# One VectorE instruction instead of two for the rests of a half of turned probabilities, and another layout of their buffer

## The chip, the cores and the metric

One core of a Trainium2 chip runs the whole program. The metric is the time of one execution on the device in microseconds. Five engines work side by side and meet through semaphores only: TensorE (PE in the rows; PEld is its weight load), VectorE (DVE), ScalarE (ACT), GpSimd (POOL), and SyncE (SP), which issues transfers.

## What is computed

A layer over 4 sequences of 2048 tokens with 256 features: "talking heads" attention with 16 heads of 16 features, whose logits and probabilities are each mixed over the heads, then a layer norm, a soft mixture of experts and a second layer norm. The attention is where the time goes:

```python
logits = jnp.einsum('bhid,bhjd->bhij', q, k) * SCALE
logits = jnp.einsum('bhij,gh->bgij', logits, Wpre)
attn = jax.nn.softmax(logits, axis=-1)
attn = jnp.einsum('bhij,gh->bgij', attn, Wpost)
out = jnp.einsum('bhij,bhjd->bhid', attn, v)
```

## The kernel before

**Tiles and slots.** A tile is 8 queries by 16 heads, which are the 128 partitions, against all 2048 keys. A sequence has 16 passes (`it`) of 16 tiles (`t`), so there are 4 × 16 × 16 = 1024 tiles. Every engine runs the same loop over slots, one slot per tile, and each works through its own list in the order in which the code is written; only semaphores tie them. In slot T the scores and the softmax of tile T are made, and the probabilities of tile T-2 are turned.

**A slot on each engine.** A slot has two halves, A (`hf` 0, the first 1024 keys) and B (`hf` 1).

- TensorE: `scores(T, 0)` (24 matmuls into `psS`), `turn(T-2, 0)` (48 small matmuls into `psP`), `scores(T, 1)`, `turn(T-2, 1)`. A turn multiplies the probabilities with the mixed post weights, so that keys become partitions. It fills both banks of `psP`: bank `ih` 0 takes the first four of the tile's eight queries, bank 1 the last four. There is one `psP`, so the next turn must wait until both banks are read (`s_ml`).
- ScalarE: for half A `mixed_high` of bank 0 and of bank 1 (line 694: `psP` rounded to float16, into the buffer `PT`, which is the tensor `big` in the rows), then `exps(T, 0)` (line 675) and `highs(T, 0)` (line 704); for half B the same with `exps(T, 1)`, `factor` (line 685) and `highs(T, 1)`.
- VectorE: `half_max(T, 0)` (line 867, 1024 scores), `recip` (898), `mixed_low` of bank 0 and of bank 1 for half A (line 878: what the rounding to float16 left over, `psP` minus the high part), `low(T-1, 1)` (line 906, 512 wide), `half_max(T, 1)`, `mixed_low` twice for half B, `low(T, 0)` (line 906, 1024 wide). `exps` waits for `half_max` (`s_nb`).
- GpSimd: mixed queries, softmax weights and a part of `low`.

Each `mixed_low(c)` waits for `mixed_high(c)` of its own bank (`s_mh`). So in a half four instructions read `psP`: ScalarE bank 0, ScalarE bank 1, VectorE bank 0, VectorE bank 1, and VectorE can be at bank 0 while ScalarE is at bank 1.

**Slots with more in them.** After 8 tiles `PT` is full, and TensorE multiplies it with the values (`output`, line 1282, 256 matmuls in four pieces) in the slots `t % 8 == 2`, the first piece already within the scores of half A. VectorE copies the result out (`out_copy`, line 889) in the slots `t % 8 == 3`. The row work (projection `y`, layer norm, routing) of earlier passes is put into slots by two tables:

```python
FIRST = dict(bias=1, y=4, residual=10, root1=(11, 4))
LATER = dict(norm=2, root2=(3, 4), turn_u=5, logits=6, keep=10, weigh=10, combine=10, turn_c=11)
```

Seven of the 16 slots of a pass (0, 7, 8, 12, 13, 14 and 15) hold none of this on TensorE or VectorE. They are called plain below.

## Time and profile before

| | |
|---|---|
| median of 3 runs | 8362.6 us (8351.86 to 8367.09) |
| profiled execution | 8358.64 us, its span 8356.8 us |
| TensorE busy | 7996.8 us, 96% of the span |
| VectorE busy | 7605.1 us, 91% |
| ScalarE busy | 6848.0 us, 82% |
| GpSimd busy | 6046.9 us, 72% |
| instructions of line 878 (VectorE) | 4096, mean 679 ns |

Busy shares tell which engines are near their limit on average; they don't tell which wait ends last in a given slot. Timelines list the start and the length of each instruction; two neighbours on one engine overlap in the records by their tails, so the pace of an engine is read from start to start. "x2" marks two merged instructions, whose length is that from the first's start to the second's end.

### The profile page before, as it was taken

What the parts mean: (1) busy time and instruction counts of PE and PEld (TensorE: products, weight loads), DVE (VectorE), ACT (ScalarE), POOL (GpSimd) and SP (SyncE); (2) the same over time, 40 slices, a digit from 0 to 9 for tenths busy, and PEclk for the clock granted to TensorE, in tenths of its full rate; (3) what the DMA queues carried; (4) which work ended last, traced back from release to release, by engine and by line L of the source; (5) the groups of instructions that cost most, each with busy time, mean ns of one, the idle gap of its engine ahead of it and who ended that gap; (6) DMA issues with size and microseconds to landing.
All of it is one profiled execution on the core that took longest, in us unless ns stands there. A gap on an engine that the chain in (4) does not pass through costs nothing.

```text
span 8356.8 us, 449859 instructions
## 1 busy us (share of the span) xinstructions
PE 7996.8 (96%) x182764; PEld 4649.9 (56%) x182764; DVE 7605.1 (91%) x13390; ACT 6848.0 (82%) x11648; POOL 6046.9 (72%) x12006
## 2 busy tenths in 40 slices
PE   7999999998899999999889999999979999999997
PEld 4555555555555555555545555555554555555554
DVE  7999999997899999999789999999978999999996
ACT  5888888886688888888568888888857888888884
POOL 6777777774677777777477777777737777777773
PEclk9999999998999999999899999999989999999998
DMA  1011111112101111111211111111121011011112
GB/s 53 23 28 27 26 26 27 26 27 91 34 24 27 27 26 26 27 28 26 89 35 25 26 27 26 27 26 27 26 88 36 25 26 28 25 27 26 27 26 93
DMA packets 265756, 284.04 MB, mean 34 GB/s; under 512 B 41089, under 2 KB 252673, under 8 KB 261377
## 3 DMA queue, kind: packets, MB, share of 16 engines
q1 hardware_dynamic: 263680, 255.07, 11.3%
q8 instruction: 1462, 23.95, 1.2%
q14 instruction: 614, 5.02, 0.2%
HBM read 78.75 MB, written 39.85 MB: 14 GB/s over the span
## 4 chain that ended last, share of the span: by engine, by line
PE 73%; DVE 12%; issue 10%; POOL 1%; ACT 1%; DVEq 1%; DMA 0%; SPq 0%; POOLq 0%; ACTq 0%
PE psS L1248 47%; PE psP L1267 15%; PE psO L1282 6%; DVE big L878 5%; DVE pl L906 2%; DVE spare L867 2%; PE psM L1293 1%; ACT big L694 1%; DVE ot L889 1%; PE psS L1378 1%; PE psM L1308 1%; PE psS L1407 1%; PE psS L1209 0%; DVE nb L867 0%; PE psS L1196 0%
## 5 line engine op out<-in xcount | busy, mean ns | idle before, releaser
L1248 PE MATMUL psS<-KH,AX 64*128 64x512 f16 x32768 | 3928.4, 377 | 52.0 <-DMA AX<-AX 50.1
L694 ACT ACTIVATE big<-psP 128x512 f16<-128x512 f32 x4096 | 2222.4, 595 | 826.2 <-PE psP L1267 822.9
L878 DVE SCALAR_TENSOR_TENSOR big<-psP,big 128x512 f16<-128x512 f32 x4096 | 2613.9, 679 | 175.5 <-ACT big L694 174.0
L675 ACT ACTIVATE pr<-psS,nb 128x1024 f32<-128x1024 f32 x2048 | 2289.7, 1118 | 192.9 <-DVE nb L867 190.1
L1248 PEld LDWEIGHTS psS<-KH,AX 64*128 64x128 f16 x32768 | 1451.5, 95 | 1513.5 <-DMA AX<-AX 51.7
L704 ACT ACTIVATE ph<-pr 128x1024 f16<-128x1024 f32 x2048 | 2166.8, 1058 | 32.3
L1248 PE MATMUL psS<-KL,AX 64*128 64x512 f16 x16384 | 2106.3, 377 | 0.0
L906 DVE TENSOR_TENSOR pl<-pr,ph 128x1024 f16<-128x1024 f32 (+1 forms) x2048 | 2078.3, 1015 | 0.0
L1267 PE MATMUL psP<-rh,ph 64*128 64x64 f16 x32768 | 1671.7, 191 | 131.4 <-DVE big L878 112.0
L1267 PEld LDWEIGHTS psP<-rh,ph 64*128 64x128 f16 x32768 | 1468.7, 95 | 557.9 <-DVE big L878 395.9
L1267 PE MATMUL psP<-rl,ph 64*128 64x64 f16 x32768 | 1667.0, 191 | 4.7 <-issue 4.3
L1267 PE MATMUL psP<-rh,pl 64*128 64x64 f16 x32768 | 1667.4, 191 | 4.0 <-issue 3.7
L567 POOL TENSOR_SCALAR tot<-sums,ff 128x1 f32<-128x1 f32 x1024 | 758.6, 741 | 1109.1 <-ACT ff L685 1104.9
L1267 PEld LDWEIGHTS psP<-rl,ph 64*128 64x128 f16 x32768 | 1463.1, 95 | 108.7 <-issue 6.1
L1267 PEld LDWEIGHTS psP<-rh,pl 64*128 64x128 f16 x32768 | 1463.6, 95 | 8.0 <-issue 7.4
L867 DVE CUSTOM_DVE_ANT_0 spare<-psS,lift 128x1024 f16<-128x1024 f32 x1024 | 1247.0, 1218 | 208.2 <-PE psS L1248 208.0
L867 DVE CUSTOM_DVE_ANT_0 spare<-psS,lift,nb 128x1024 f16<-128x1024 f32 x1024 | 1310.7, 1280 | 102.5 <-PE psS L1248 95.1
L1248 PEld LDWEIGHTS psS<-KL,AX 64*128 64x128 f16 x16384 | 806.8, 94 | 963.4 <-issue 3.4
L558 POOL TENSOR_TENSOR pl<-pr,ph 128x512 f16<-128x512 f32 x1024 | 1217.9, 1189 | 0.0
L486 POOL TENSOR_TENSOR at<-Q,wpre_q 128x128 f32<-128x128 f32 x2048 | 784.0, 402 | 6.9 <-POOL AX L499 5.0
L499 POOL TENSOR_TENSOR AX<-at,AX 128x256 f16<-128x256 f32 x1024 | 687.0, 671 | 2.6
L591 POOL CAST rh<-rp 128x128 f16<-128x128 f32 x1024 | 653.9, 639 | 7.6 <-POOL rp L582 6.5
(137 smaller groups left out, 6286.4 us busy)
## 6 DMA issues: line engine op xcount, KB each, us to landing
AX<-AX SPq DMA_DIRECT2D x2048, 64.0 KB, 2.0
ph<-in_xT SPq DMA_DIRECT2D x16, 512.0 KB, 8.7
xr<-in_x SPq DMA_DIRECT2D x64, 128.0 KB, 2.3
Q<-in_w SPq DMA_DIRECT2D x8, 1024.0 KB, 7.2
out<-V SPq DMA_DIRECT2D x16, 512.0 KB, 3.7
d_x<-x SPq DMA_DIRECT2D x60, 128.0 KB, 2.0
d_xn<-xn SPq DMA_DIRECT2D x60, 128.0 KB, 2.0
d_lg<-lg SPq DMA_DIRECT2D x60, 128.0 KB, 2.0
```

Of the source, the lines that this page charges most:

```text
L486: g.tensor_tensor(v, Q[:, :, bass.ds(i0, HQ)].unsqueeze(2).broadcast_to([P, KT, H, HQ]), wpre_q[:, :].unsqueeze(1).unsqueeze(3).broadcast_ ...
L499: g.tensor_tensor(AX[:, t % TG, 0:KT, 1, :], at[:, :, :], AX[:, t % TG, 0:KT, 0, :], ALU.subtract).then_inc(s_A, 1)
L558: g.tensor_tensor(pl[:, t % 2, NL:N], pr[:, t % 2, NL:N], ph[:, t % 2, NL:N], ALU.subtract).then_inc(s_plg, 1)
L567: g.tensor_scalar(tot[:, p:p + 1], sums[:, p, 0:1], ff[:, p, 0:1], sums[:, p, 1:2], ALU.mult, ALU.add).then_inc(s_tot, 1)
L675: a.activation(pr[:, p, h * N2:(h + 1) * N2], psS[:, 2 * h:2 * h + 2, :].rearrange("p c n -> p (c n)"), ACT.Exp, bias=nb[:, p, h:h + 1], s ...
L694: a.activation(PT[:, hf * JH:(hf + 1) * JH, :, 0, i0:i0 + HQ], psP[:, ih, :].rearrange("p (j g i) -> p j g i", j=JH, g=H), ACT.Copy, scale ...
L704: a.activation(ph[:, t % 2, cs], pr[:, t % 2, cs], ACT.Copy).then_inc(s_ph, 1)
L867: v.tensor_tensor_reduce(out=spare[:, :], in0=psS[:, 2 * h:2 * h + 2, :].rearrange("p c n -> p (c n)"), in1=lift[:, 0:1].broadcast_to([P, ...
L878: v.scalar_tensor_tensor(out=PT[:, js, :, 1, i0:i0 + HQ], in0=psP[:, ih, :].rearrange("p (j g i) -> p j g i", j=JH, g=H), scalar=MDROP, in ...
L906: v.tensor_tensor(pl[:, t % 2, cs], pr[:, t % 2, cs], ph[:, t % 2, cs], ALU.subtract)\
L1248: mm = pe.matmul(psS[:, 2 * hp + half, :], AX[rows, k8, kq, s_, :], K_[rows, kq, hp, :], start=n == 0, stop=n == len(steps) - 1, tile_posi ...
L1267: mm = pe.matmul(psP[:, ih, j * HP:(j + 1) * HP], p_[rows, t % 2, cs], r_[rows, t % 4, hf, :], start=n == 0, stop=n == 2, tile_position=(i ...
```

## The change

`mixed_low` is called once per half instead of twice. It waits until ScalarE has done both banks, and makes the rests of both banks in one instruction of 1024 elements per partition. For its output to be one regular pattern over both banks, the buffer `PT` is laid out anew: key half `f` and query half `h` come first, then key tile, head, high/rest, query. The other edits follow from that: the order of the queries inside a group of 64 changes (GpSimd reads `Q` at another offset), the output matmuls read their 128 columns as two runs of 64, `out_copy` writes its result back in two runs, and `s_ml` counts two per tile.

```diff
@@ -106,7 +106,7 @@
 
         big = sb("big", [P, JT * H * GI])
 
-        PT = big[:, :].bitcast(F16).rearrange("p (j g s i) -> p j g s i", j=JT, g=H, s=2)
+        PT = big[:, :].bitcast(F16).rearrange("p (f h j g s i) -> p f h j g s i", f=2, h=2, j=JH, g=H, s=2)
         KH = sb("KH", [P, KQ, NP, CW], F16)
         KL = sb("KL", [P, KQ, NP, CW], F16)
         V = sb("V", [P, JT, H, 2, HD], F16)
@@ -480,7 +480,7 @@
                         g.wait_ge(s_S, T * 2 - (TG - 1) * 2)
                     g.wait_ge(s_A, T * 4 + 1)
                     for h in range(2):
-                        i0 = it * (TI * QI) + (t * QI + h * HQ)
+                        i0 = it * (TI * QI) + t // TG * GI + h * (GI // 2) + t % TG * HQ
                         v = at[:, :, h * HP:(h + 1) * HP].rearrange("p k (g i) -> p k g i", g=H)
                         apart(g)
                         g.tensor_tensor(v, Q[:, :, bass.ds(i0, HQ)].unsqueeze(2).broadcast_to([P, KT, H, HQ]),
@@ -690,8 +690,8 @@
                     a.wait_ge(s_D, T * 2 + hf + 1 + 1)
                     if t % TG == 0:
                         a.wait_ge(s_F, Gd * NC + 2 * hf + 2)
-                    i0 = (t % TG) * QI + ih * HQ
-                    a.activation(PT[:, hf * JH:(hf + 1) * JH, :, 0, i0:i0 + HQ],
+                    i0 = (t % TG) * HQ
+                    a.activation(PT[:, hf, ih, :, :, 0, i0:i0 + HQ],
                                  psP[:, ih, :].rearrange("p (j g i) -> p j g i", j=JH, g=H),
                                  ACT.Copy, scale=MDROP).then_inc(s_mh, 1)
 
@@ -869,16 +869,13 @@
                                            op0=ALU.add, op1=ALU.min,
                                            accum_out=nb[:, t % 2, h:h + 1]).then_inc(s_nb, 1)
 
-                def mixed_low(T, t, c):
-
-                    v.wait_ge(s_mh, T * NC + c + 1 + 1)
-                    hf, ih = c // 2, c % 2
-                    i0 = (t % TG) * QI + ih * HQ
-                    js = slice(hf * JH, (hf + 1) * JH)
-                    v.scalar_tensor_tensor(out=PT[:, js, :, 1, i0:i0 + HQ],
-                                           in0=psP[:, ih, :].rearrange("p (j g i) -> p j g i", j=JH, g=H),
-                                           scalar=MDROP, in1=PT[:, js, :, 0, i0:i0 + HQ],
-                                           op0=ALU.mult, op1=ALU.subtract).then_inc(s_ml, 1)
+                def mixed_low(T, t, hf):
+
+                    v.wait_ge(s_mh, T * NC + 2 * hf + 2 + 1)
+                    i0 = (t % TG) * HQ
+                    high, rest = (PT[:, hf, :, :, :, k, i0:i0 + HQ].rearrange("p h j g i -> p (h j g) i") for k in range(2))
+                    v.scalar_tensor_tensor(out=rest, in0=psP[:, :, :].rearrange("p h (a i) -> p (h a) i", i=HQ),
+                                           scalar=MDROP, in1=high, op0=ALU.mult, op1=ALU.subtract).then_inc(s_ml, 1)
 
                 def out_copy(Gd, half, R, part):
 
@@ -886,8 +883,8 @@
                         v.wait_ge(s_F, (Gd + 1) * NC + NC)
                         v.wait_ge(s_y, R + 1)
                     qs = slice(part * GQ // 2, (part + 1) * GQ // 2)
-                    ins = v.tensor_reduce(ot[:, qs, half * GI:(half + 1) * GI],
-                                          psO[:, qs.start * P:qs.stop * P].rearrange("p (q s i) -> p q i s", s=2, i=GI),
+                    ins = v.tensor_reduce(ot[:, qs, half * GI:(half + 1) * GI].rearrange("p q (h i) -> p q h i", h=2),
+                                          psO[:, qs.start * P:qs.stop * P].rearrange("p (q h s i) -> p q h i s", h=2, s=2, i=GI // 2),
                                           X, ALU.add)
                     ins.then_inc(s_oc, 1)
 
@@ -1078,7 +1075,6 @@
                     rows(it, t, 0)
                     if two:
                         mixed_low(T - 2, t_2, 0)
-                        mixed_low(T - 2, t_2, 1)
                     copied(it, t, first, 0)
                     rows(it, t, 1)
                     if one:
@@ -1087,8 +1083,7 @@
                         half_max(T, t, 1)
                     rows(it, t, 2)
                     if two:
-                        mixed_low(T - 2, t_2, 2)
-                        mixed_low(T - 2, t_2, 3)
+                        mixed_low(T - 2, t_2, 1)
                     copied(it, t, first, 1)
                     if live:
                         low(T, t, 0, first and t < 2)
@@ -1258,7 +1253,7 @@
                         pe.wait_ge(s_pl, T * 2 + 2 + 1)
                         pe.wait_ge(s_plg, T + 1 + 1)
                     if not fresh:
-                        pe.wait_ge(s_ml, T * NC + 2 * hf + 1)
+                        pe.wait_ge(s_ml, T * 2 + hf + 1)
                     for j in range(JH):
                         cs = slice((hf * JH + j) * P, (hf * JH + j + 1) * P)
                         for n, (p_, r_) in enumerate(((ph, rh), (ph, rl), (pl, rh))):
@@ -1274,13 +1269,13 @@
                     if 0 in pieces:
                         pe.wait_ge(s_oc, Gd * 2 + 1)
                     for c in pieces:
-                        pe.wait_ge(s_ml, Tn * NC - NC + c // 2 * 2 + 2 + 1)
+                        pe.wait_ge(s_ml, Tn * 2 - 2 + c // 2 + 1 + 1)
                         for j in range(c * JC, (c + 1) * JC):
                             for q in range(GQ):
                                 for w in range(4):
                                     g_ = 4 * q + w
                                     mm = pe.matmul(psO[32 * w:32 * w + 32, q * P:(q + 1) * P],
-                                                   V[:, j, g_, :, :], PT[:, j, g_, :, :],
+                                                   V[:, j, g_, :, :], PT[:, j // JH, :, j % JH, g_, :, :],
                                                    start=j == 0 and q == 0, stop=j == JT - 1,
                                                    skip_group_check=True, tile_position=(0, 32 * w))
                         mm.then_inc(s_F, 1)
```

VectorE in one plain slot, from the maximum of half A on, before the change (line 898 is the reciprocal, `nb` the maxima; plain semaphore and register rows left out):

```order
L867 ISA spare,nb<-psS,lift 128x1024 [waits s_S,s_nb]
L867 ISA nb 128x1
L898 RECIPROCAL rc<-tot 128x1 [waits s_tot]
L878 SCALAR_TENSOR_TENSOR big<-psP,big 128x128x4 [waits s_mh]
L878 SCALAR_TENSOR_TENSOR big<-psP,big 128x128x4 [waits s_mh]
L906 TENSOR_TENSOR pl<-pr,ph 128x512 [waits s_D,s_ph]
L867 ISA spare,nb<-psS,lift,nb 128x1024 [waits s_S,s_nb]
L867 ISA nb 128x1
L878 SCALAR_TENSOR_TENSOR big<-psP,big 128x128x4 [waits s_mh]
L878 SCALAR_TENSOR_TENSOR big<-psP,big 128x128x4 [waits s_mh]
L906 TENSOR_TENSOR pl<-pr,ph 128x1024 [waits s_D,s_ph]
```

And the same place in the changed kernel:

```order
L867 ISA spare,nb<-psS,lift 128x1024 [waits s_S,s_nb]
L867 ISA nb 128x1
L895 RECIPROCAL rc<-tot 128x1 [waits s_tot]
L877 SCALAR_TENSOR_TENSOR big<-psP,big 128x256x4 [waits s_mh]
L903 TENSOR_TENSOR pl<-pr,ph 128x512 [waits s_D,s_ph]
L867 ISA spare,nb<-psS,lift,nb 128x1024 [waits s_S,s_nb]
L867 ISA nb 128x1
L877 SCALAR_TENSOR_TENSOR big<-psP,big 128x256x4 [waits s_mh]
L903 TENSOR_TENSOR pl<-pr,ph 128x1024 [waits s_D,s_ph]
```

Of each pair of rows of line 878 one row of twice the elements stays, in the same place between its neighbours; its wait on `s_mh` is now for both banks.

TensorE at the change from the scores of half B to the turn of half B, before:

```order
L1248 MATMUL psS<-KH,AX 128x512 [waits s_exp]
L1248 MATMUL psS<-KH,AX 128x512 x15
L1248 MATMUL psS<-KL,AX 128x512 x8
L1261 REGISTER_ALU [waits s_plg,s_pl]
L1267 MATMUL psP<-rh,ph 128x64 [waits s_ml]
L1267 MATMUL psP<-rh,ph 128x64
```

And in the changed kernel:

```order
L1243 MATMUL psS<-KH,AX 128x512 [waits s_exp]
L1243 MATMUL psS<-KH,AX 128x512 x15
L1243 MATMUL psS<-KL,AX 128x512 x8
L1262 MATMUL psP<-rh,ph 128x64 [waits s_ml,s_plg,s_pl]
L1262 MATMUL psP<-rh,ph 128x64
L1262 MATMUL psP<-rl,ph 128x64 x2
```

The first matmul of a turn still waits for `s_ml`, and no matmul changes its place; the waits for `s_plg` and `s_pl` now stand on that matmul instead of on a row ahead of it.

## Rows read from the trace of the kernel before

**Rows 1.** The page: busy times, then the granted TensorE clock in 40 slices.

```profile
...
PE 7996.8 (96%) x182764; PEld 4649.9 (56%) x182764; DVE 7605.1 (91%) x13390; ACT 6848.0 (82%) x11648; POOL 6046.9 (72%) x12006
...
PEclk9999999998999999999899999999989999999998
...
```

**Rows 2.** Groups by line and form; after the bar: busy us, mean ns, idle before.

```profile
...
L878 DVE SCALAR_TENSOR_TENSOR big<-psP,big 128x512 f16<-128x512 f32 x4096 | 2613.9, 679 | 175.5 <-ACT big L694 174.0 <-issue 0.7
...
L694 ACT ACTIVATE big<-psP 128x512 f16<-128x512 f32 x4096 | 2222.4, 595 | 826.2 <-PE psP L1267 822.9
...
L906 DVE TENSOR_TENSOR pl<-pr,ph 128x1024 f16<-128x1024 f32 x1024 | 1272.6, 1243 | 0.0
L867 DVE CUSTOM_DVE_ANT_0 spare<-psS,lift 128x1024 f16<-128x1024 f32 x1024 | 1247.0, 1218 | 208.2 <-PE psS L1248 208.0
...
L1282 PE MATMUL psO<-big,V 128*32 128x128 f16 x32768 | 561.5, 221 | 14.5 <-issue 14.1
...
```

**Rows 3.** Line 878: what it waited for, then who waited for it (us, times).

```profile
...
  ACT big L694: 174.0, 190
...
  PEld psP L1267: 395.9, 917
  PE psP L1267: 112.0, 219
...
```

**Rows 4.** Busy time of each engine in stretches of one pass.

```profile
...
1260.40:1300.91 40.51, 40.10 (x897) 22.15 (x897) 40.23 (x67) 39.25 (x67) 36.11 (x72) 1.00 0.12 30
1300.91:1342.14 41.23, 40.45 (x959) 23.68 (x948) 36.61 (x65) 32.48 (x56) 29.25 (x63) 1.00 0.11 29
...
```

**Rows 5.** Timeline of VectorE in slots 12 and 13 (start us, us, what).

```profile
...
1260.40 1.21 DVE L867 CUSTOM_DVE_ANT_0 spare<-psS,lift 128x1024 f16<-128x1024 f32 x1
...
1261.61 1.26 DVE L878 SCALAR_TENSOR_TENSOR big<-psP,big 128x512 f16<-128x512 f32 x2
...
1264.60 1.28 DVE L878 SCALAR_TENSOR_TENSOR big<-psP,big 128x512 f16<-128x512 f32 x2
1265.80 1.21 DVE L906 TENSOR_TENSOR pl<-pr,ph 128x1024 f16<-128x1024 f32 x1
1266.93 1.22 DVE L867 CUSTOM_DVE_ANT_0 spare<-psS,lift 128x1024 f16<-128x1024 f32 x1
...
```

**Rows 6.** Timeline of ScalarE in slots 12 and 13.

```profile
...
1261.65 1.11 ACT L675 ACTIVATE pr<-psS,nb 128x1024 f32<-128x1024 f32 x1 [0.23 <-DVE nb L867]
...
1262.89 1.06 ACT L704 ACTIVATE ph<-pr 128x1024 f16<-128x1024 f32 x1
1263.85 1.09 ACT L694 ACTIVATE big<-psP 128x512 f16<-128x512 f32 x2
...
1267.14 1.09 ACT L694 ACTIVATE big<-psP 128x512 f16<-128x512 f32 x2
```

**Rows 7.** Timeline of TensorE, a first matmul that waited, and an unhindered one.

```profile
...
1262.93 0.20 PE L1267 MATMUL psP<-rh,ph 64*128 64x64 f16 x2 [0.41 <-DVE big L878]
...
1266.24 0.19 PE L1267 MATMUL psP<-rh,ph 64*128 64x64 f16 x2
```

**Rows 8.** Chain that ended last, the same stretch (start us, us, what).

```profile
...
1263.81 2.59 PE psS L1248 x24
1266.40 0.70 PE psP L1267 x48
...
```

**Rows 9.** Timeline of VectorE, end of slot 6 and slot 7.

```profile
...
1339.80 1.29 DVE L878 SCALAR_TENSOR_TENSOR big<-psP,big 128x512 f16<-128x512 f32 x2 [0.94 <-ACT big L694]
1341.01 1.22 DVE L906 TENSOR_TENSOR pl<-pr,ph 128x1024 f16<-128x1024 f32 x1
1342.14 1.22 DVE L867 CUSTOM_DVE_ANT_0 spare<-psS,lift 128x1024 f16<-128x1024 f32 x1
...
```

**Rows 10.** Timeline of ScalarE at the same place.

```profile
...
1339.17 1.09 ACT L694 ACTIVATE big<-psP 128x512 f16<-128x512 f32 x2 [1.01 <-PE psP L1267]
...
```

**Rows 11.** Timeline of TensorE, first matmul of the next turn.

```profile
...
1344.85 0.19 PE L1267 MATMUL psP<-rh,ph 64*128 64x64 f16 x2
...
```

## The prediction, made before the changed kernel was run

> **What bounds the kernel now.** I read the page first: TensorE 96% busy, VectorE 91%, ScalarE 82% [rows 1]. That is near balance, so the order of waits inside a slot decides, not a share. The granted clock is at its higher level, 2.4 GHz, nearly everywhere (nines in the page's line of tenths, an 8 three or four times) [rows 1], so it plays no part.
>
> Second, the stretches of one pass of 16 slots. Slots 12 to 1, six slots of which five are plain, take 40.51 us, with TensorE busy for 40.10 and VectorE for 40.23 of them [rows 4]: both full. In slots 2 to 6 (outputs, projection, routing) VectorE is busy for 36.61 of 41.23 us [rows 4]: there it waits, and whatever lag it had is absorbed.
>
> Third, the chain that ended last. In plain slots it is TensorE alone: 2.59 us of scores, 0.70 us of turn [rows 8], so 3.29 us a half and **6.58 us a slot** as TensorE's floor. VectorE, from one maximum of half A to the next, needs 1266.93 - 1260.40 = 6.53 us [rows 5]. The two are 0.05 us apart, and a gain on VectorE can show only where VectorE is behind.
>
> Fourth, who waits for line 878: TensorE's matmuls 112.0 us in 219 waits, its weight loads 395.9 us in 917 [rows 3]. The loads run ahead of the matmuls, so the true loss is the 112.0 us, 1.3% of the span. The same waits are the place where a later end of line 878 shows at once.
>
> **The change, part by part.**
>
> *The instruction itself.* Two of 512 elements take 1.26 us from the first's start to the second's end, and the next VectorE instruction starts 1265.80 - 1264.60 = 1.20 us after the first [rows 5]. The trace has no such instruction of 1024. The nearest rows: `low` of 1024 elements is followed after 1266.93 - 1265.80 = 1.13 us and takes 1.21 [rows 5]. I take 1.13 from start to start and 1.21 to its end: 0.07 us less per half on VectorE, 0.05 to 0.06 earlier done if it could start at the same time. Bounds: no saving at all (1.20), or, if the longer pattern ran at the 679 ns for 512 of [rows 2] throughout, 1.36.
>
> In the Trainium skill, Perfetto Trace Analysis, section Optimizing Scalar/DVE Operations, an operation on PSUM carries some 125 ns of overhead, and grouping pays if the engine is saturated. By that the saving would be 0.125 us per half instead of 0.07, and the sum below would come out near 45 us lower.
>
> *The start.* This is what the change costs. Before, the first `mixed_low` needs only the first `mixed_high`, which takes 0.60 us [rows 2]; after, it needs both, 1.09 us [rows 6]. The signal adds 0.03 us: at the end of slot 6 VectorE was waiting, ScalarE began at 1339.17 and VectorE at 1339.80, 0.63 us later, of which 0.60 are the instruction [rows 9, 10]. So the earliest start moves from 0.63 to 1.12 us after ScalarE's first. And VectorE uses that room now: in slot 12 ScalarE's pair runs from 1263.85 to 1264.94, and VectorE starts at 1264.60 [rows 5, 6], 0.37 us earlier than the changed kernel could.
>
> *Does TensorE feel it?* From a turn's first matmul to `mixed_high` pass 1267.14 - 1266.24 = 0.90 us [rows 6, 7], and the next turn is due 3.29 us after the first [rows 8], so 2.39 us after `mixed_high` begins. A turn that waited began 0.06 us after line 878 ended (1261.61 + 1.26 = 1262.87, then 1262.93) [rows 5, 7]. In the changed kernel the shortest way is 1.12 + 1.21 + 0.06 = 2.39 us. It just fits, with no slack left: every further delay on VectorE or ScalarE lengthens TensorE's time.
>
> *Two loops, once round per slot.* (H is the instruction of line 694, M line 878.)
>
> Loop 1, VectorE and ScalarE: maximum of half A to the exponential 1261.65 - 1260.40 = 1.25; exponential to `highs` 1.24; `highs` to H of half B 0.96 [rows 5, 6]; H to M; M; `low` 1.13; maximum again. Before: 1.25 + 1.24 + 0.96 + 0.63 + 1.20 + 1.13 = 6.41, under TensorE's 6.58 and VectorE's 6.53. After: 1.25 + 1.24 + 0.96 + 1.12 + 1.13 + 1.13 = **6.83**.
>
> Loop 2, VectorE and TensorE: M of half B 1.13; `low` 1.13; maximum and reciprocal 1261.61 - 1260.40 = 1.21; M of half A to its end 1.21; 0.06; turn to H 0.90; H to M 1.12: 6.76 after, where before it was 1.20 + 1.13 + 1.21 + 1.26 + 0.06 + 0.90 + 0.63 = 6.39.
>
> Both pass TensorE's floor, and the longer one sets the pace: a plain slot goes from 6.58 to 6.83 us, +0.25, although VectorE has 0.14 us less to do in it.
>
> *Where it counts.* From M of slot 12 to that of slot 1 there are five steps of a slot, from slot 7 to 9 two: 7 × 0.25 = 1.75 us a pass. Getting into the loop costs once each time. At slot 7 M of half B starts at 1339.17 + 1.12 = 1340.29 instead of 1339.80, `low` 0.42 later than 1341.01, the maximum 0.42 later at 1342.56, M of half A 1.21 after that at 1343.77, ends at 1344.98, turn at 1345.04 instead of 1344.85: +0.2 [rows 9 to 11]. I take 0.20 at slots 3 and 11 too, 0.60 a pass; the rest of the slots with extra TensorE work gives VectorE room, so I count nothing there. That cover is the 4.6 us of idle VectorE in slots 2 to 6 [rows 4].
>
> Sum: (1.75 + 0.60) × 64 passes = **+150 us**. Against the execution's own 8358.6 us that is 8509; the median of the runs lies 4 us above that execution, so I predict **8513 us**.
>
> *The other edits.* GpSimd's offset, ScalarE's output pattern (same runs of four, other strides) and the two runs of `out_copy` I cost at nothing; `out_copy` is few and short, and its slots are those where TensorE carries outputs just before. The output matmuls read two runs of 64 columns: 32768 matmuls [rows 2], all on TensorE's path. No row shows a moving operand in two runs. The bounds are 0 and, if every matmul of the group took twice as long, its whole 561.5 us; the number of columns stays the same, so I take 0, and leave the rest to the tail of the larger loss.
>
> **Rivals.**
>
> *Faster (0.12): VectorE's throughput decides.* If ScalarE's second H is done by the time VectorE arrives, only the shorter instruction is left. That is so from a lag of 1.12 us behind H's start; the rows show 1264.60 - 1263.85 = 0.75 [rows 5, 6]. VectorE is behind TensorE in about four slots a pass (after the copies: TensorE's 0.41 us wait in slot 12 [rows 7]); 4 × 0.14 × 64 = 36 us gained, 8327 us. The grouping rule above speaks for this one.
>
> *No change (0.07): the delays are swallowed.* It needs about 0.25 us of slack per slot in a link that I call tight, for instance if exponentials could start earlier than the 1.25 us. Then 8363 us. Against: ScalarE already waited 0.23 us for the maximum here [rows 6].
>
> *A smaller loss (0.12).* If only loop 2 holds, a plain slot costs 0.18: (7 × 0.18 + 0.6) × 64 = 119 us; with entries absorbed too, 80 us: 8400 to 8455 with the surroundings.
>
> *A larger loss (0.07).* The pattern at 1.36 us gives a loop of 7.06, +0.48: (7 × 0.48 + 0.9) × 64 = 273 us, 8636 us.
>
> The same page and section of the Trainium skill has the opposite advice where Scalar or Vector cause bubbles on other engines: break instructions up, so that work is done sooner. By that this change goes the wrong way; the 112.0 us of waits for line 878 are such bubbles, and the rule agrees with my sign, not with a size.
>
> **How the numbers follow.** My forecast has 0.62. Its own range: no saving in the instruction adds 0.07 to loop and entries, 10 × 0.07 × 64 = 45 us, so up to 8575; a link 0.08 us looser takes the same off, 8455. The range over the cases, 8370 to 8600, leaves out the faster one, a part of no change and the top of the larger loss. A measurement of this kernel tells 0.2%, 17 us, from no change. Slower: 0.62 + 0.12 + 0.07 = 0.81; within 0.2%: 0.07; faster: 0.12.
>
> **What would show it.** Line 878 (now 877) has 2048 instructions of some 1.20 us, and waits for `mixed_high` thousands of times a few tenths long instead of 190 times [rows 3]. VectorE's busy time falls by about 100 to 300 us while its idle time grows by more. TensorE waits for that line far longer than 112 us. A plain slot takes 6.83 us, and slots 1, 9 and 2 to 6 stay as they are. ScalarE's exponential of half A waits for the maximum in nearly every plain slot. I am wrong if plain slots stay at 6.58 (the loops have slack), or if the instruction takes well over 1.25 us, or if matmuls of line 1282 (now 1277) get longer.

## The result: 1.9% slower

The changed kernel takes 8518.3 us (median, 8514.1 to 8525.75) against 8364.85 us of the kernel before on the same chip: a ratio of 1.0188, 95% interval 1.017 to 1.0205. The prediction was 8513 us. The profiled execution has a span of 8513.8 us, 157.0 us more than before, at the same mean granted clock (0.984 in both).

The page of the changed kernel, busy times and the changed line (after the bar: busy us, mean ns, idle before):

```profile
...
PE 8124.4 (95%) x182764; PEld 4659.5 (55%) x182764; DVE 7525.6 (88%) x11342; ACT 6895.9 (81%) x11648; POOL 6218.4 (73%) x12006
...
L877 DVE SCALAR_TENSOR_TENSOR big<-psP,big 128x1024 f16<-128x1024 f32 x2048 | 2489.2, 1215 | 539.1 <-ACT big L694 533.8
...
```

Against [rows 1, 2]: VectorE is busy for 79 us less (7605.1 to 7525.6), its line for 125 us less (2613.9 to 2489.2), and the kernel is slower. The instruction saved about what was costed, and more than that was lost elsewhere. The view of the line says where (us, times; first what it waited for, then who waited for it):

```profile
...
  ACT big L694: 533.8, 1084
...
  PEld psP L1262: 294.7, 779
  PE psP L1262: 91.7, 171
...
```

It now waits 1084 times for ScalarE, 533.8 us in all, where before it was 190 times and 174.0 us [rows 3]. The rows of TensorE have to be read with care. Its matmuls wait 91.7 us for the line, less than the 112.0 of before, and its weight loads 294.7 instead of 395.9. The loss is not there, because part of the waiting now ends in an instruction of TensorE's sequencer: the trace has 1024 event instructions with the wait for `s_ml` ahead of the turns of half B, and none before. What stands behind such an instruction is booked as "issue": 494.4 us of the weight loads' idle time have that name in the changed kernel, 24.5 before. The row of these loads, before (group by form) and in the changed kernel (page):

```profile
...
L1267 PEld LDWEIGHTS psP<-rh,ph 64*128 64x128 f16 x32768 | 1468.7, 95 | 557.9 <-DVE big L878 395.9 <-issue 24.5 <-POOL rl L596 15.1
...
```

```profile
...
L1262 PEld LDWEIGHTS psP<-rh,ph 64*128 64x128 f16 x32768 | 1463.8, 95 | 864.0 <-issue 494.4
...
```

An experiment below puts the wait back onto the load, and the row comes back with it.

Slots 12 to 1 and slots 2 to 6 of the same pass, as in [rows 4] (stretch, its length, then busy us of TensorE, its loads, VectorE, ScalarE, GpSimd):

```profile
...
1286.14:1327.88 41.74, 41.28 (x905) 22.80 (x902) 39.47 (x56) 39.49 (x66) 36.50 (x72) 1.00 0.11 28
1327.88:1369.49 41.61, 41.03 (x970) 23.89 (x960) 36.86 (x56) 33.14 (x57) 30.01 (x63) 1.00 0.11 29
...
```

Slots 12 to 1 took 40.51 us and take 41.74; VectorE is idle for 2.27 us of it, where it had 0.28. Slots 2 to 6 took 41.23 and take 41.61. Over the 52 passes that are not the first two or the last of a sequence, a pass went from 120.54 to 123.00 us (from start to start of line 867's form without `nb`, the maximum of half A); 2.46 × 64 = 157 us, the whole difference of the two spans.

A plain slot, slot 13 of that pass: VectorE,

```profile
...
1293.01 1.22 DVE L867 CUSTOM_DVE_ANT_0 spare<-psS,lift 128x1024 f16<-128x1024 f32 x1
...
1294.23 1.20 DVE L877 SCALAR_TENSOR_TENSOR big<-psP,big 128x1024 f16<-128x1024 f32 x1
...
1297.61 1.22 DVE L877 SCALAR_TENSOR_TENSOR big<-psP,big 128x1024 f16<-128x1024 f32 x1 [0.37 <-ACT big L694]
1298.75 1.22 DVE L903 TENSOR_TENSOR pl<-pr,ph 128x1024 f16<-128x1024 f32 x1
1299.88 1.22 DVE L867 CUSTOM_DVE_ANT_0 spare<-psS,lift 128x1024 f16<-128x1024 f32 x1
```

ScalarE,

```profile
...
1294.27 1.11 ACT L675 ACTIVATE pr<-psS,nb 128x1024 f32<-128x1024 f32 x1 [0.25 <-DVE nb L867]
...
1295.51 1.06 ACT L704 ACTIVATE ph<-pr 128x1024 f16<-128x1024 f32 x1
1296.49 1.08 ACT L694 ACTIVATE big<-psP 128x512 f16<-128x512 f32 x2
...
```

and the chain that ended last at the same place:

```profile
...
1289.59 2.59 PE psS L1243 x24
1292.17 0.72 PE psP L1262 x48
1292.89 2.59 PE psS L1243 x24
1295.48 0.10 issue
1295.58 0.88 PE psP L1262 x48
1296.45 2.59 PE psS L1243 x24
...
```

From maximum to maximum pass 1299.88 - 1293.01 = **6.87 us**; before it was 6.53 in [rows 5], and 6.58 as a mean over all plain slots of the 52 passes. Line 877 of half B starts at 1297.61, 1.12 us after ScalarE's first `mixed_high` (1296.49), and the maximum before it was done 0.37 us earlier: VectorE stands still, then `low` and the next maximum come late. In all 364 plain slots of the 52 passes line 877 waits in half B and never in half A. In the chain the 2.59 us of scores are as in [rows 8], but every second turn takes 0.10 and 0.88 us instead of 0.70 (the other 0.72). That is TensorE's wait in small pieces.

### The profile page after: what moved, and what is told of

Same layout as the page of the kernel before. It is cut to its first block, busy times and chain, and to the rows that moved or that the text cites. A ratio compares the mean times of both kernels' runs of the same rounds, so it can differ in the third digit from the quotient of the medians.

```text
span 8513.8 us, 444739 instructions
## 1 busy us (share of the span) xinstructions
PE 8124.4 (95%) x182764; PEld 4659.5 (55%) x182764; DVE 7525.6 (88%) x11342; ACT 6895.9 (81%) x11648; POOL 6218.4 (73%) x12006
## 4 chain that ended last, share of the span: by engine, by line
PE 82%; issue 8%; DVE 5%; ACT 2%; POOL 1%; DVEq 0%; DMA 0%; ACTq 0%; SPq 0%; POOLq 0%
PE psS L1243 53%; PE psP L1262 17%; PE psO L1277 6%; DVE big L877 2%; PE psM L1288 1%; ACT big L694 1%; DVE spare L867 1%; PE psS L1373 1%; PE psS L1402 1%; PE psM L1303 1%; ACT ph L704 1%; DVE pl L903 0%; PE psS L1204 0%; DVE ot L886 0%; PE psS L1191 0%
## 5 line engine op out<-in xcount | busy, mean ns | idle before, releaser
L877 DVE SCALAR_TENSOR_TENSOR big<-psP,big 128x1024 f16<-128x1024 f32 x2048 | 2489.2, 1215 | 539.1 <-ACT big L694 533.8
L1243 PEld LDWEIGHTS psS<-KH,AX 64*128 64x128 f16 x32768 | 1511.8, 94 | 1467.6 <-issue 54.5
L567 POOL TENSOR_SCALAR tot<-sums,ff 128x1 f32<-128x1 f32 x1024 | 1159.2, 1132 | 1092.7 <-ACT ff L685 1090.7
L1262 PEld LDWEIGHTS psP<-rh,ph 64*128 64x128 f16 x32768 | 1463.8, 95 | 864.0 <-issue 494.4
L1262 PE MATMUL psP<-rh,ph 64*128 64x64 f16 x32768 | 1686.7, 191 | 162.0 <-DVE big L877 91.7
L1243 PEld LDWEIGHTS psS<-KL,AX 64*128 64x128 f16 x16384 | 835.9, 94 | 935.6 <-issue 5.6
L558 POOL TENSOR_TENSOR pl<-pr,ph 128x512 f16<-128x512 f32 x1024 | 1197.4, 1169 | 0.0
L499 POOL TENSOR_TENSOR AX<-at,AX 128x256 f16<-128x256 f32 x1024 | 741.2, 724 | 2.6
L591 POOL CAST rh<-rp 128x128 f16<-128x128 f32 x1024 | 621.5, 607 | 7.6 <-POOL rp L582 6.5
```

Of the source, the lines that this page charges most:

```text
L499: g.tensor_tensor(AX[:, t % TG, 0:KT, 1, :], at[:, :, :], AX[:, t % TG, 0:KT, 0, :], ALU.subtract).then_inc(s_A, 1)
L558: g.tensor_tensor(pl[:, t % 2, NL:N], pr[:, t % 2, NL:N], ph[:, t % 2, NL:N], ALU.subtract).then_inc(s_plg, 1)
L567: g.tensor_scalar(tot[:, p:p + 1], sums[:, p, 0:1], ff[:, p, 0:1], sums[:, p, 1:2], ALU.mult, ALU.add).then_inc(s_tot, 1)
L877: v.scalar_tensor_tensor(out=rest, in0=psP[:, :, :].rearrange("p h (a i) -> p (h a) i", i=HQ), scalar=MDROP, in1=high, op0=ALU.mult, op1=A ...
L1243: mm = pe.matmul(psS[:, 2 * hp + half, :], AX[rows, k8, kq, s_, :], K_[rows, kq, hp, :], start=n == 0, stop=n == len(steps) - 1, tile_posi ...
L1262: mm = pe.matmul(psP[:, ih, j * HP:(j + 1) * HP], p_[rows, t % 2, cs], r_[rows, t % 4, hf, :], start=n == 0, stop=n == 2, tile_position=(i ...
```

## Experiments

The theory (T): the late start of the merged instruction lengthens two loops that go round once per slot, and the layout is free. (Loop 1 runs over VectorE and ScalarE, loop 2 over VectorE and TensorE, as summed in the prediction.) Rivals: the layout is what costs (R1); a merged half costs its share whichever half it is (R2); the longer instruction or something else on VectorE costs (R3). Each run's ratio is to the kernel before in the same call.

| run | median us | ratio (95% interval) | plain slot, us |
|---|---|---|---|
| before | 8362.3 to 8367.1 | 1 | 6.58 |
| changed | 8518.3 | 1.0188 (1.017 to 1.0205) | 6.87 |
| layout only | 8370.2 | 1.0002 (0.9993 to 1.0012) | 6.58 |
| delay only | 8600.9 | 1.0280 (1.0263 to 1.0297) | 6.91 |
| both merged, old count | 8534.1 | 1.0204 (1.0187 to 1.0221) | 6.90 |
| first half merged, old count | 8400.1 | 1.0038 (1.0025 to 1.0050) | 6.74 |
| second half merged, old count | 8591.0 | 1.0269 (1.0252 to 1.0287) | 6.92 |
| both merged, old count, even `low` | 8519.4 | 1.0187 (1.0170 to 1.0204) | 6.82 |
| both merged, old count, high merged | 8514.4 | 1.0179 (1.0162 to 1.0196) | 6.86 |
| changed, wait apart | 8475.0 | 1.0132 (1.0115 to 1.0149) | 6.83 |
| the same, even `low` | 8461.7 | 1.0114 (1.0097 to 1.0131) | 6.69 |
| the same, even `low`, high merged | 8380.5 | 1.0020 (1.0010 to 1.0029) | 6.59 |
| first half merged, clean | 8373.0 | 1.0011 (1.0001 to 1.0020) | 6.58 |
| before, even `low` | 8333.4 | 0.9958 (0.9944 to 0.9973) | 6.58 |

The last column is slot 8, from maximum to maximum, as a mean over the same 52 passes. Of the twelve expectations two had the measured time in their range (layout only; first half merged, clean). The direction was right in most, the size often not, and the text below says why as far as the traces show it.

**Layout only.** The new buffer with everything that follows from it, but one instruction per bank:

```diff
-    v.wait_ge(s_mh, T * NC + 2 * hf + 2 + 1)
+    for ih in range(2):
+        v.wait_ge(s_mh, T * NC + 2 * hf + ih + 1 + 1)
+        v.scalar_tensor_tensor(out=PT[:, hf, ih, :, :, 1, i0:i0 + HQ], ...).then_inc(s_ml, 1)
```

Expected:

> Only the layout of the buffer of turned probabilities is changed, with all that follows from it (query order, output matmuls that read two runs of 64 columns, the copies out); VectorE still makes the rests of each bank in an instruction of its own, each waiting for its own bank only. Theory of the loops: the layout costs nothing, 8365 us within 20. Rival, that the layout is what costs (two runs per output matmul, other strides): 8450 to 8520 us.

Measured 8370.2 us, the kernel before. R1 falls. The output matmuls, whose two runs of 64 columns no row of before could price, cost nothing (group row, after the bar: busy us, mean ns, idle before):

```profile
...
L1286 PE MATMUL psO<-big,V 128*32 128x128 f16 x32768 | 561.1, 221 | 14.2 <-issue 13.7
...
```

It was 561.5 us, 221 ns in [rows 2].

**Delay only.** The kernel before with one line changed:

```diff
-                    v.wait_ge(s_mh, T * NC + c + 1 + 1)
+                    v.wait_ge(s_mh, T * NC + c // 2 * 2 + 2 + 1)
```

> The kernel before, with its layout and its two instructions per half, but each waits until ScalarE has done both banks. Theory of the loops: the late start is the whole loss and the saving is lost too. Loop 1 is 1.25 + 1.24 + 0.96 + 1.12 + 1.20 + 1.13 = 6.90 us per plain slot, 0.03 above the 6.87 of the changed kernel, and the slots of VectorE are 0.14 longer: 8530 to 8570 us. Rival, that the loss comes from the layout or from the longer instruction: 8365 us within 20.

Measured 8600.9 us, 30 above the range. The direction settles the main question: without the layout and without the long instruction the late start alone costs 2.8%, more than the whole change. The plain slot is where the sum put it (6.91 for 6.90). The difference to the changed kernel is mostly in slots 3 and 11, where VectorE copies outputs: 7.69 and 7.70 us here, 7.23 and 7.24 in the changed kernel. So the changed kernel is 0.46 us better in each, (0.46 + 0.46) × 64 = 59 us of the 83 between the two, where I had only counted 0.14 per slot. What makes these two slots shorter is told in the last section.

**One half merged.** First half A, then half B, in a family in which `s_ml` keeps its old count and a merged instruction raises it by two:

```diff
+                    if MERGED[hf]:
+                        v.wait_ge(s_mh, T * NC + 2 * hf + 2 + 1)
+                        v.scalar_tensor_tensor(...).then_inc(s_ml, 2)
+                        return
```

> The new layout; one instruction for both banks in half A only, two in half B. Theory of the loops: the delayed start counts only where loop 1 and loop 2 pass, from ScalarE's to VectorE's work in half B, and half A is not on it. Loop 1 stays at 6.41, loop 2 at about 6.35, TensorE's 6.58 us decides again, and VectorE has 0.07 us less to do: 8330 to 8370 us. Rival, that every merged half costs its share: 8440 us.

> The new layout; one instruction for both banks in half B only, two in half A. Theory of the loops: nearly the whole loss. Loop 1 6.83, loop 2 6.81, so a plain slot takes 6.83 us: 8490 to 8520 us. Rival, that every merged half costs its share: 8440 us.

Measured 8400.1 and 8591.0 us, so both above their ranges, but not alike: 33 and 224 us over the kernel before. R2 had 8440 for both. The loss sits with half B, as the loops say, since both hold the link from ScalarE's to VectorE's work in half B. A part of why both are too high the next run shows.

**Both merged, old count.** The same family with both halves merged, meant to free TensorE's wait:

> The changed kernel, but s_ml counts four per tile as before, two for each instruction. Then the wait for s_ml stands alone on the first matmul of a turn of half B, and not with two other waits; nothing else differs. Theory: in the changed kernel these three waits share one place, VectorE's end of the rests reaches TensorE 0.15 instead of 0.06 us later, and loop 2 with it is 6.85; without it loop 1 sets 6.83 us per plain slot: 8485 to 8505 us. Rival, that loop 1 alone sets the pace and the place of the wait does not matter: 8518 us within 10.

Measured 8534.1 us: 16 us more than the changed kernel, which neither theory had. The intervals of the two ratios overlap, but the plain slot says the same (6.90 against 6.87). Timelines of VectorE and of ScalarE in this run, half B of a plain slot:

```profile
...
2684.50 1.23 DVE L879 SCALAR_TENSOR_TENSOR big<-psP,big 128x1024 f16<-128x1024 f32 x1 [0.35 <-ACT big L695]
...
```

```profile
...
2683.34 1.06 ACT L695 ACTIVATE big<-psP 128x512 f16<-128x512 f32 x2
...
```

ScalarE's pair ends at 2683.34 + 1.06 = 2684.40, VectorE starts 0.10 us later. In the changed kernel it is 1296.49 + 1.08 = 1297.57 and 1297.61, 0.04 later. The trace has an event instruction of VectorE's sequencer with the wait for `s_mh` ahead of the instruction at 2684.50, and none in the changed kernel. The only thing that differs on VectorE is that `s_ml` is raised by two, and the count fits: 2048 such event instructions here, 1024 with one half merged, none in any kernel that raises `s_ml` by one. TensorE's wait for `s_ml` is back on the weight load, as meant. So the whole family carries 0.06 us more in the link that both loops hold: loop 1 is 1.26 + 1.24 + 0.96 + 1.06 + 0.10 + 1.14 + 1.13 = 6.89, and 6.90 was measured. Its runs are comparable with each other only. Within it, half A merged or not makes 57 us the other way (8591.0 to 8534.1), most of it again in slots 3 and 11 (7.63 to 7.24 us). Half B merged alone was not run with `s_ml` raised by one; its 224 us hold the family's 0.06 us and these two slots as well.

**Changed, wait apart.** The same question with `s_ml` raised by one. `apart` raises a semaphore and does nothing else. Put between the waits, ahead of the turns of both halves, it takes the other waits onto itself and leaves the one for `s_ml` on the weight load:

```diff
                         pe.wait_ge(s_plg, T + 1 + 1)
+                    apart(pe)
                     if not fresh:
                         pe.wait_ge(s_ml, T * 2 + hf + 1)
```

> The changed kernel, with TensorE's wait for s_ml ahead of the turn of half B standing alone on the first weight load (the two other waits, long fulfilled, go ahead of it in an instruction of their own). In the changed kernel's trace an event instruction of the sequencer with the wait for s_ml stands ahead of the load, and the turn starts 0.15 us after VectorE's end instead of 0.06. Theory: loop 2 falls from 6.87 to 6.79 and loop 1 sets 6.84 us per plain slot: 8495 to 8510 us. Rival: the place of the wait costs nothing that counts, 8518 us within 6.

Measured 8475.0 us, 43 us better than the changed kernel, more than I gave it. (The kernels before of the two calls differ by 1 us.) The chain that ended last in this run:

```profile
...
2666.43 0.87 PE psP L1263 x48
2667.30 2.59 PE psS L1243 x24
2669.89 0.77 PE psP L1263 x48
2670.66 2.59 PE psS L1243 x24
2673.26 0.01 issue
2673.26 0.87 PE psP L1263 x48
...
```

Turns of 0.77 to 0.87 us, and no "issue" of 0.10 left. The plain slot is 6.83 us: loop 1 exactly. And the waits have their name again (us, times, longest):

```profile
...
PEld psP L1263 <- DVE big L877: 758.6, 1555, 2.6
...
PE psP L1263 <- DVE big L877: 76.1, 120, 2.4
...
```

where the changed kernel showed 294.7 for the loads. The trace has no event instruction with `s_ml` ahead of a turn any more; all 2044 waits are on the load. The plain slots' 0.04 us is under half of the gain. Slots 1 and 9, which are in no loop, became 0.19 and 0.10 us shorter: (0.19 + 0.10) × 64 = 19 us. That it is the same wait there is not shown.

**Even `low`.** Both loops contain the `low` of 1024 elements, so VectorE's two instructions are made equal:

```diff
-                    cs = (slice(0, N2), slice(N2, NL))[h]
+                    cs = (slice(0, NL // 2), slice(NL // 2, NL))[h]
```

with the waits for `s_pl` moved to match. First in the family of the old count, then in the kernel before as a control, then cleanly:

> As the run before, and VectorE's two instructions of low have 768 elements each instead of 1024 and 512 (waits for s_pl moved to fit). Theory of the loops: both loops contain the one of 1024, and lose 0.27 us: 6.56 and 6.49, under TensorE's 6.58. Plain slots take 6.58 us again, and slots where VectorE decides gain: 8320 to 8375 us. Rival, that VectorE is slow for another reason (more waits, the longer instruction): little changes, 8480 to 8510 us.

> The kernel before, with 768 and 768 elements in low. Control for the run before: TensorE's 6.58 us sets plain slots anyway, so the loops' theory expects 8365 us within 25. If it is much faster, the even split is worth something by itself.

> As the run before, with two instructions of 768 elements in low instead of 1024 and 512. The first try of this split carried an event instruction ahead of each rest instruction (start 0.10 instead of 0.04 us after ScalarE's end), which is gone here. Theory: both loops fall by 0.27 us to about 6.57 and 6.52; what is left is the direct way of a half, turn to ScalarE 0.91, ScalarE's pair 1.09, signal 0.04, rests 1.23, signal 0.06: 3.33 us, 6.65 per plain slot instead of 6.84 and of 6.58 in the kernel before: 8390 to 8440 us. Rival, that the loops are not what binds: 8480 to 8510 us.

Measured 8519.4, 8333.4 and 8461.7 us. The first missed widely. I had only looked at the two loops, and not at the direct way of a half: from a turn to ScalarE, to VectorE, and to the next turn, since there is one `psP`. By the sum in the expectation of the third run it takes 3.33 us as soon as the instruction is merged, and 3.39 with the 0.06 of the old count; both are over TensorE's 3.29. The third stays 22 us above its range, and gains 13 us where 35 or more was expected. The loops were indeed shortened: the seven plain slots of a pass lose 0.81 us together (slot 8 went from 6.83 to 6.69), and 6.69 is near the direct way's 2 × 3.33. But slots 3 and 11 became 0.45 us longer each, which takes back (0.45 + 0.45) × 64 = 58 us; their `low` of VectorE takes 1.41 and 1.37 us as a mean, 0.69 in the run before it. The first run has the same (7.24 and 7.23 to 7.62 and 7.67 us). The control gained 0.4% by itself, which I had not expected to be measurable; it is the fastest kernel of this study, faster than before and changed.

**High merged.** ScalarE, too, takes both banks in one instruction, so that the direct way gets shorter: in the family of the old count, and on top of the clean even `low`.

```diff
-                    i0 = (t % TG) * HQ
-                    a.activation(PT[:, hf, ih, :, :, 0, i0:i0 + HQ],
-                                 psP[:, ih, :].rearrange("p (j g i) -> p j g i", j=JH, g=H),
+                    if ih:
+                        return
+                    i0 = (t % TG) * HQ
+                    a.activation(PT[:, hf, :, :, :, 0, i0:i0 + HQ].rearrange("p h j g i -> p (h j g) i"),
+                                 psP[:, :, :].rearrange("p h (a i) -> p (h a) i", i=HQ),
```

> The changed kernel with the old count (third run before this), and ScalarE too makes the high parts of both banks in one instruction of 1024 elements. Theory of the loops: from the start of ScalarE's work to VectorE's pass some 1.02 + 0.03 us instead of 1.12, both loops lose 0.07 us, a plain slot takes 6.76: 8450 to 8470 us. Rival: no gain where ScalarE waits for a maximum anyway, 8485 to 8505 us.

> As the run before, and ScalarE makes the high parts of both banks in one instruction of 1024 elements (1.02 us in the earlier run that had it, instead of 1.09 for the pair). Theory: the direct way of a half falls to 0.91 + 1.02 + 0.04 + 1.23 + 0.06 = 3.26 us, under TensorE's 3.29, so plain slots take TensorE's 6.58 us, and slots bound by VectorE gain: 8330 to 8375 us. Rival, that something else is left behind the loops: 8400 us or more.

Measured 8514.4 and 8380.5 us. The first is 20 us under the same family without it, and 44 above its range. It raises `s_mh` by two, and now ScalarE's own wait is in an event instruction (1792 of 2048 times): ScalarE's earliest start is 0.965 us after a turn's first matmul, in the traces of before, changed and five other runs it is 0.905. That takes back the 0.06 that the single instruction saves. The second run raises `s_mh` by one; it is 5 us above its range. With VectorE's merged instruction still in both halves, 17 us are left to the kernel before, and 47 to the control with the same even `low` (8333.4). So R3 can't hold for more than that; and the run with the delay only, which has no long instruction and loses more than the whole, speaks against it directly. VectorE in two halves of it:

```profile
...
1268.51 0.94 DVE L905 TENSOR_TENSOR pl<-pr,ph 128x768 f16<-128x768 f32 x1
1269.38 1.21 DVE L869 CUSTOM_DVE_ANT_0 spare<-psS,lift 128x1024 f16<-128x1024 f32 x1
...
1270.76 1.22 DVE L879 SCALAR_TENSOR_TENSOR big<-psP,big 128x1024 f16<-128x1024 f32 x1
1271.90 1.09 DVE L905 TENSOR_TENSOR pl<-pr,ph 128x768 f16<-128x768 f32 x1
1272.92 1.27 DVE L869 CUSTOM_DVE_ANT_0 spare<-psS,lift,nb 128x1024 f16<-128x1024 f32 x1
...
1274.12 1.21 DVE L879 SCALAR_TENSOR_TENSOR big<-psP,big 128x1024 f16<-128x1024 f32 x1
1275.26 0.99 DVE L905 TENSOR_TENSOR pl<-pr,ph 128x768 f16<-128x768 f32 x1
1276.17 1.21 DVE L869 CUSTOM_DVE_ANT_0 spare<-psS,lift 128x1024 f16<-128x1024 f32 x1
...
```

In half B line 879 starts at 1274.12, as soon as the maximum is done, with no idle time between them; in the changed kernel there were 0.37 us. What is left in these slots (6.79 us here, 6.59 in slot 8) is seen in the two `low`, 1.09 and 0.99 us for 768 elements, where the one at 1268.51 took 0.94. Both start while an instruction of GpSimd runs, and both end 0.8 us after that one's end (1272.19 and 1275.43); the last section has the rule.

**First half merged, clean.** Half A merged and half B split, each instruction raising `s_ml` by one, with the wait kept apart as above:

> One instruction for both banks in half A only, two in half B, as in an earlier run, but s_ml is raised by one each time, so that no event instruction stands ahead of the rests (that run had one, and plain slots of 6.53 to 6.79 us). Theory: half A is on neither loop's critical link, loops 6.41 and about 6.35; only the direct way of half A, 3.33 us, passes TensorE's 3.29 by 0.04: 8345 to 8385 us. Rival, that a merged half costs half of the whole loss: 8440 us.

Measured 8373.0 us, 0.1% above the kernel before. A merged instruction in half A costs next to nothing. R2 falls with it.

## Why the prediction was right, step by step

- **The instruction.** Costed at 1.13 us from start to start and 1.21 to its end; it takes 1298.75 - 1297.61 = 1.14 and a mean of 1.215. By the 125 ns of the Trainium skill (Perfetto Trace Analysis, Optimizing Scalar/DVE Operations) VectorE's pace of two half instructions, 1.20 us, would have fallen to an estimated 1.08; the trace gives 0.06 us saved, so here the rows were the better guide. The prediction's "near 45 us lower" for that rival is too much by its own sum: (0.125 - 0.07) × 10 × 64 = 35 us.
- **The start.** 1.12 us after ScalarE's first, measured 1297.61 - 1296.49 = 1.12. That this alone makes a loss of at least this size is shown by the run with the delay only; that the layout is free, by the first run.
- **Which loop.** Loop 1 was 6.83, loop 2 6.76, and I said the longer one sets the pace. The longer one was loop 2. The mis-sized term is the signal from VectorE to TensorE, taken as 0.06 from a turn of before. In the changed kernel the count of `s_ml` lets three waits gather on one weight load, an event instruction with the wait for `s_ml` goes ahead of it, and the turn of half B starts some 0.09 us later: 6.76 + 0.09 = 6.85. With every link read from the plain slot above, loop 2 is 1.14 + 1.13 + 1.22 + 1.20 + 0.15 + 0.91 + 1.12 = 6.87, which is the slot. With the wait apart the slot is 6.83, loop 1 as summed. My plain slot (+0.25) was 0.04 too low for that reason.
- **Where it counts.** Per pass, by the 52 passes: slots 10 to 1 +1.42 us, for which I had 0.2 + 5 × 0.25 = 1.45; slots 2 to 4 +0.13, for 0.2; slots 5 to 9 +0.91, for 0.2 + 2 × 0.25 = 0.7. In all 2.46 for 2.35, and 157 us for 150. That the sum comes so close is in part luck. The seven plain slots grew by 2.02 us, for 1.75. The other nine grew by 0.44, for 0.60, but as what is left of large terms that I did not have: +0.55, +0.35 and +0.31 us in slots 2, 5 and 10, which is 77 us of the run, and -0.45 each in slots 3 and 11, which is 58 us the other way. In the run with the delay only, where slots 3 and 11 stay as they were, the same sum gave a range that ends 31 us under the measured time.
- **The cover.** VectorE's idle time in slots 2 to 6 (4.75 us after, 4.62 before) did not shrink, and these slots took 0.58 us longer in all (mean of the 52 passes), where I had only the 0.2 of one entry. So they hid less than said.
- **What would show it.** The line has 2048 instructions: right. VectorE less to do: right, but by 79 us and not by 100 to 300; its idle time grew by 236, as said by more. ScalarE's exponential of half A waits for the maximum in all 364 plain slots of the 52 passes: right. Slots 2 to 6 "stay as they are": wrong, as above; 1 and 9 did within 0.05 us. "Waits thousands of times": it was 1084, mostly because the start in half A is late by the loop anyway and finds ScalarE done; in plain slots only half B waits. "TensorE waits for that line far longer than 112 us": true of its time, wrong of the row, which went to "issue".
- **The rivals.** Faster needed VectorE to come 1.12 us behind ScalarE's first; it does so in half A only. Splitting that case off, half A merged alone, gave 1.0011, so not even there was something to gain. The second rule of that page of the Trainium skill, to break instructions up where ScalarE or VectorE cause bubbles on other engines, agrees with the result: the split kernel is the faster one. The page gives it for engines that aren't saturated, and VectorE was busy for 91%; the runs tell no more of it than the sign. Two of the bounds don't follow from their sums: the smaller loss of 119 us is 8482 us and lies in the forecast's own range, not in 8400 to 8455, and the steps of 45 and 51 us around 8513 give 8462 to 8558, not 8455 to 8575. The measured time is far from both.

What stays open: how much of the +0.55 and +0.31 us of slots 2 and 10 comes from the late start and how much from VectorE's `low` against GpSimd (below), and what half B merged alone costs without the event instruction. The 0.1 us by which the version with even `low` and high merged misses TensorE's floor in slots 12 to 15 is as large as what its `low` there takes too long (1.02 to 1.07 us as a mean for 0.94 to 0.95).

## What to carry to other kernels

Two instructions that read two banks let the second engine start on the first bank while the first engine is at the second. Merging them saves one fixed cost (0.06 us here) and gives up that overlap (0.49 us here), so ask whether the instruction's start or its length is on a loop, and sum that loop before and after. A buffer that is written and read once per half period gives a third, direct loop: writer, first reader, second reader, writer; sum it as well. When a semaphore's count is changed, look at how the waits are gathered on the instructions behind it: 0.04 us per slot and 43 us in all came from that here, with no line of the computation touched. And before a sum of durations is trusted, look at which instructions of VectorE change their length with what GpSimd does at that moment.

## What the runs showed of the hardware that was not expected

- Waits gathered on one instruction: three on a weight load made the turn start about 0.15 us after VectorE's end instead of 0.06; and raising a semaphore by two moved that instruction's own wait into an event instruction ahead of it, and it starts 0.10 us instead of 0.04 after the releasing engine's end. It is so in every trace that has such an instruction: a wait of VectorE moves there when it raises `s_ml` by two, one of ScalarE when it raises `s_mh` by two.
- VectorE's `low` of 512 elements in slot 11, before and after. Timelines of VectorE, before,

```profile
...
1255.40 1.20 DVE L906 TENSOR_TENSOR pl<-pr,ph 128x512 f16<-128x512 f32 x1
...
```

and after:

```profile
...
2661.23 0.68 DVE L903 TENSOR_TENSOR pl<-pr,ph 128x512 f16<-128x512 f32 x1
...
```

Between the starts of GpSimd's `AX` subtraction beside it, before,

```profile
...
1255.38 0.68 POOL L499 TENSOR_TENSOR AX<-at,AX 128x256 f16<-128x256 f32 x1
...
```

and after,

```profile
...
2661.34 1.10 POOL L499 TENSOR_TENSOR AX<-at,AX 128x256 f16<-128x256 f32 x1
...
```

there is a shift of a few hundredths of a us relative to `low` (0.02 ahead of it before, 0.11 behind it after), and one of the two is slow each time: `low` 1.20 us and the subtraction 0.68 before, `low` 0.68 and the subtraction 1.10 after. The trace shows no wait at either. The ends fit an engine that stands still for the other: before, `low` ends at 1256.60, 0.54 us after GpSimd's subtraction is done at 1255.38 + 0.68 = 1256.06; after, the subtraction ends at 2662.44, 0.53 after `low` is done at 2661.91. It is what makes slots 3 and 11 better in the changed kernel than any sum of durations gave. No run was made to set the two starts apart, but the 14 kernels do it by themselves. In their 52 passes there are 23296 `low`. The 8325 that start while no instruction of GpSimd runs are all short (at most 0.69 us for 512 elements, 0.96 for 768, 1.22 for 1024). The 2241 of 512 elements that start with 0.2 us or more of a GpSimd instruction still to come end 0.55 us after that one's end as a median, 98% of them within 0.54 to 0.55, whatever the offset. So the change also made a `low` longer, in slot 5, where it took 0.68 us before. VectorE and GpSimd there, in the changed kernel:

```profile
...
1356.82 1.18 DVE L903 TENSOR_TENSOR pl<-pr,ph 128x512 f16<-128x512 f32 x1
...
```

```profile
...
1356.78 0.67 POOL L499 TENSOR_TENSOR AX<-at,AX 128x256 f16<-128x256 f32 x1
...
```

  The subtraction is done at 1357.45, `low` at 1358.00. The mean `low` went from 1.16 to 0.70 us in slots 3 and 11, from 1.10 to 0.77 in slot 10, from 0.90 to 1.44 in slot 2 and from 0.68 to 1.18 in slot 5; over the whole run the ones of 512 elements take 818.1 us for 805.8 before. The change moved these collisions to other slots and did not remove them.

  The Trainium skill has such a rule (SBUF — State Buffer, section "SBUF: two separate sides"): VectorE's operations with two inputs in SBUF and GpSimd's operations that read SBUF lock one pair of ports between them, and whichever starts first holds it for the whole instruction. `low` has two such inputs, `pr` and `ph`, and in both traces the one that starts first is the quick one: the rows agree with it, and so do the counts over the 14 traces. I had not weighed it in the prediction, where it would have put a coin's toss of 0.5 us on each of the slots in which the two starts lie close.
